# Where the weight pieces of a first mixture-of-experts loop are stored and loaded: SP's queue against ACT's queue

## The reference

```python
# block 0: 8 experts, hidden 512
h = jnp.einsum('nd,ehd->neh', xf, w1)
g = jnp.einsum('nd,ehd->neh', xf, w3)
eo = jnp.einsum('neh,edh->ned', jax.nn.silu(h) * g, w2)
out = jnp.einsum('ned,ne->nd', eo, comb)
...
# block 1: 8 experts, hidden 1024
for i in range(e):
    h = jax.nn.silu(xf @ w1[i] + b1[i])
    y = h @ w2[i] + b2[i]
    out = out + y * comb[:, i:i + 1]
```

## Time and profile before

| | us |
|---|---|
| median of 3 executions | 1332.95 (1329.78 to 1335.05) |
| the profiled execution | 1337.71 |
| its span, first to last instruction | 1336.0 |

### The profile page before, as it was taken

One profiled execution on the slowest core, in us unless ns is written; L12 is line 12 of the kernel. 1 busy time (PEld: TensorE's weight loads), 2 busy tenths in 40 slices (PEclk: granted clock), 3 DMA queues, 4 the chain that ended last, 5 costly groups with the idle time before them and its releaser, 6 DMA issues.

```text
span 1336.0 us, 26989 instructions
## 1 busy us (share of the span) xinstructions
PE 949.3 (71%) x7185; PEld 796.7 (60%) x7185; DVE 843.2 (63%) x1909; ACT 567.7 (42%) x1227; POOL 411.5 (31%) x478
## 2 busy tenths in 40 slices
PE   5210376837598888888860388457999999999943
PEld 4100265715587777777750277416888888888832
DVE  6999498898655544554545776683555555555545
ACT  5265423347575555555540023283444333443312
POOL 1285000000045444554540150003444444444310
PEclk8655596556799999999995595557999999999975
DMA  7067204913757666676677502104442442443257
GB/s 253 1 203 209 67 0 135 318 51 103 224 158 203 192 194 184 193 195 197 185 209 220 199 0 79 48 0 100 133 142 74 139 139 77 146 129 75 76 164 251
DMA packets 189423, 189.19 MB, mean 142 GB/s; under 512 B 91264, under 2 KB 158536, under 8 KB 189256
## 3 DMA queue, kind: packets, MB, share of 16 engines
q1 hardware_dynamic: 171032, 145.71, 36.6%
q0 software_dynamic: 14000, 38.82, 10.0%
q10 hardware_dynamic: 4352, 4.20, 0.9%
HBM read 119.98 MB, written 49.28 MB: 127 GB/s over the span
## 4 chain that ended last, share of the span: by engine, by line
PE 40%; DMA 29%; DVE 11%; issue 10%; ACT 4%; SPq 3%; DVEq 1%; POOLq 1%; POOL 0%; ACTq 0%
PE bank L713 15%; PE bank L735 14%; DMA region<-rows_x,fetch_now 11%; DMA xt<-region 9%; DMA wreg<-in_L_ffn_w_dram 6%; PE bank L646 4%; PE bank L563 2%; DMA wreg<-rows_y 2%; ACT xt L885 2%; PE bank L618 1%; ACT wreg L835 1%; PE bank L771 1%; DVE region L1034 1%; DVE tok L1377 1%; DVE xn L1005 1%
## 5 line engine op out<-in xcount | busy, mean ns | idle before, releaser
L713 PE MATMUL bank<-xt,wreg 128*128 x3360 | 388.3, 277 | 56.3 <-DMA xt<-region 55.7
L713 PEld LDWEIGHTS bank<-xt,wreg 128*128 128x128 f16 x3360 | 329.6, 99 | 109.4 <-issue 66.1
L735 PE MATMUL bank<-wreg,region 128*128 128x256 f16 x2520 | 286.5, 273 | 0.0
L735 PEld LDWEIGHTS bank<-wreg,region 128*128 128x128 f16 x2520 | 246.6, 98 | 28.5
L917 ACT ACTIVATE region<-bank,b_t,wreg 128x256 f32<-128x256 f32 x280 | 142.7, 560 | 227.0 <-PE bank L713 227.0
L465 POOL DMA_INDIRECT region<-rows_x,fetch_now x144 | 148.0, 1028 | 197.8 <-DMA xt<-region 132.9
L507 POOL DMA_INDIRECT rows_y<-region,put_now x140 | 139.5, 996 | 196.8 <-DVE region L1362 128.8
L1354 DVE TENSOR_SCALAR region<-region,wreg 128x512 f16<-128x512 f32 x140 | 76.4, 546 | 68.9 <-ACT region L917 66.8
L563 PE MATMUL bank<-ident,xn 128*128 128x128 f32 x256 | 54.8, 374 | 88.4 <-DVE xn L1005 82.3
L1347 DVE SCALAR_TENSOR_TENSOR region<-bank,fac,region 128x256 f32<-128x256 f32 x140 | 67.6, 483 | 72.5 <-ACT region L908 71.2
L908 ACT ACTIVATE region<-bank,fac 128x256 f32<-128x256 f32 x140 | 65.6, 469 | 107.5 <-PE bank L713 106.5
(11 more groups left out here) (238 smaller groups left out, 1191.5 us busy)
## 6 DMA issues: line engine op xcount, KB each, us to landing
wreg<-in_L_ffn_w_dram SPq DMA_DIRECT2D x138, 256.0 KB, 3.0
wreg<-in_L_ffn_w_dram SPq DMA_DIRECT2D x48, 512.0 KB, 6.2
split_v<-wreg SPq DMA_DIRECT2D x35, 512.0 KB
wreg<-split_v SPq DMA_DIRECT2D x32, 512.0 KB, 6.9
wreg<-rows_y SPq DMA_DIRECT2D x48, 256.0 KB, 3.6
rows_x<-region SPq DMA_DIRECT2D x16, 512.0 KB, 3.3
wreg<-in_x_dram SPq DMA_DIRECT2D x4, 1024.0 KB, 9.4
out_dram<-xt ACTq DMA_DIRECT2D x16, 256.0 KB, 3.7
```

Source lines behind the costliest of these rows:

```text
L713: last = pe.matmul(to, block, x_cols[:, bass.ds(b, 1), :, xs_, k, :].rearrange("p j r n -> p (j r) n"), start=(k == 0 and ws_ + xs_ == 0), ...
L735: last = pe.matmul(yb[:, r * C:(r + 1) * C], lhs[:, c, r * P:(r + 1) * P], block, start=first, stop=end, skip_group_check=True)
```

## The change

The store of a piece moves from SP's order to ACT's, one piece later, and the load of a piece moves up on SP's to right behind the transposes, one piece less ahead:

- SP iteration n: transposes of tile n+2, then two one-pass loops (the loads so far; the low part of piece n-1) instead of three, then the load of piece n+1 (before: n+2). No store. Before the loop only piece 0 is loaded (before: pieces 0 and 1).
- ACT iteration n: `split_hi(n)`, then the new `move_pieces(n)`: two one-pass loops (the store before; the low part of piece n-1) and the store of piece n-1. Then the copy of tile n's result as before. One more store follows the loop, behind a wait for the last low part.
- `piece_out` moves to another place in the same buffer. In iteration 0 the store of "piece -1" writes slot 2, which POOL has filled with zeros before the loop; the real piece 31 overwrites it later.

```diff
-        piece_out = wreg[:, 26624:29696].bitcast(F16).rearrange("p (j m s n) -> p j m s n", j=3, m=2, s=2)
+        piece_out = wreg[:, 29184:32256].bitcast(F16).rearrange("p (j m s n) -> p j m s n", j=3, m=2, s=2)
...
                     load_piece(0)
-                    sp.wait_ge(piece_loaded, 32)
-                    load_piece(1)
                 for e in range(E):
                     with sp.Fori(edges[e], edges[e + 1]) as n:
                         sp.wait_ge(z_ready[f], 4 * n + 4)
                         turn_rows(f, n + 2)
                         if f == 0:
-                            for waited, each, more in ((piece_stored, 16, 0), (piece_loaded, 32, 64), (piece_lo, 1, 1)):
+                            for waited, each, more in ((piece_loaded, 32, 32), (piece_lo, 1, 0)):
                                 with sp.Fori(n, n + 1) as m:
                                     sp.wait_ge(waited, each * m + more)
-                                    sp.sem_inc(sp_passed, 1)
-                            store_piece(n)
-                            load_piece(n + 2)
+                                    sp.sem_inc(loads_passed, 1)
+                            load_piece(n + 1)
...
-            for waited, each, more in ((piece_loaded, 32, 64), (piece_stored, 16, 0), (xc_ready[0][0], 16, 32),
+            for waited, each, more in ((piece_loaded, 32, 32), (piece_stored, 16, 16), (xc_ready[0][0], 16, 32),
...
                     pool.wait_ge(peak1_ready, 1)
+                    nc.gpsimd.memset(piece_out[:, 2].rearrange("p m s n -> p (m s n)"), 0.0)
                     spread_peaks(1)
...
+            def store_last(n):
+
+                last = (n + PIECES - 1) % PIECES
+                act.dma_start(split_v[bass.ds(last // 4, 1), :, bass.ds(last % 4 * (2 * FH[1]), 2 * FH[1])].rearrange("a p n -> p (a n)"),
+                              piece_out[:, bass.ds((n + 2) % 3, 1)].rearrange("p j m s n -> p (j m s n)")).then_inc(piece_stored, 16)
...
+            def move_pieces(n):
+
+                for waited, each in ((piece_stored, 16), (piece_lo, 1)):
+                    with act.Fori(n, n + 1) as m:
+                        act.wait_ge(waited, each * m)
+                        act.sem_inc(pieces_passed, 1)
+                store_last(n)
...
                         if f == 0:
                             split_hi(n)
+                            move_pieces(n)
                             act.wait_ge(y_ready[f], n + 1)
...
             experts(0, edges)
+            with act.Fori(edges[E], edges[E] + 1) as m:
+                act.wait_ge(piece_lo, m)
+                act.sem_inc(pieces_passed, 1)
+            store_last(edges[E])
             deviation(2)
```

More of the change, by code:

```diff
@@ L264, in bass_metaformer @@
         sum_loaded, summed, peak1_ready = [sem(f"sum_loaded{j}") for j in range(3)], sem("summed"), sem("peak1_ready")
-        v_loaded, sp_passed = sem2("v_loaded"), sem("sp_passed")
+        v_loaded, pieces_passed = sem2("v_loaded"), sem("pieces_passed")
+        loads_passed = sem("loads_passed")
         stage_loaded = sem2("stage_loaded")
@@ L273, in bass_metaformer, with load_half @@
         bias_added, conv_added = sem2("bias_added"), sem2("conv_added")
+        v1_rows, v2_rows = v1.rearrange("e (k p) f -> (e k) p f", p=P), v2.rearrange("e (q c p) d -> (e q) p c d", c=2, p=P)
+        def load_half(eng, to, m, n):
+            if m == 0:
+                return eng.dma_start(to, v1_rows[bass.ds(n // 2, 1), :, bass.ds(n % 2 * 512, 512)].rearrange("a p f -> p (a f)"))
+            return eng.dma_start(to.rearrange("p (c d) -> p c d", c=2), v2_rows[bass.ds(n, 1)].rearrange("a p c d -> p (a c) d"))
         block = ctx.enter_context(nc.Block())
@@ L297, in load_stage0 @@
                              w2[bass.ds(e, 1)].rearrange("a (c p) h -> p (a c) h", p=P)).then_inc(loaded[j], 16)
[L299 to L305, removed]
             def store_rows(f, i):
@@ L327, in _ @@
                 free(sp, summed, n - 2)
-                load_half(sum_in[:, n % 3], n % 2, n // 2).then_inc(sum_loaded[n % 3], 16)
+                load_half(sp, sum_in[:, n % 3], n % 2, n // 2).then_inc(sum_loaded[n % 3], 16)
             with sp.Fori(0, HB // 2 - 1) as h:
@@ L352, in load_piece @@
                 for m in range(2):
[L353 to L358, removed]
+                    load_half(sp, piece_in[:, bass.ds(slot, 1), m].rearrange("p j n -> p (j n)"), m, piece).then_inc(piece_loaded, 16)
             def load_v(e):
```

## The result

The changed kernel takes **1360.09 us** in the median (1356.84 to 1364.61) against 1334.00 of the kernel before beside it (1329.78 to 1336.18). The ratio is 1.0197, 95% interval 1.0165 to 1.0229: slower by 26 us. The forecast was no change, 1333 us, in a range up to 1358; the case that came is the long ring.

What follows compares the result with a forecast made beforehand. Gather and transposes bound the first loop at 19.01 us per two tiles; a new ring of 19.1 would replace them. 16 pairs gave +1.4 us, the end −1.5: no change, 1333 us, range 1312 to 1358.

Steps and rivals of the forecast that it cites:

- no change: Likeliest case for the first loop: two tiles take 18.8 to 19.5 us, time stays 1333 us; chance 0.40.
- the long ring: Rival: late piece meets other traffic, ACT's added work unhidden; two tiles take 20.7 us, +25 us, 1358 us; chance 0.30.
- The direct chain: First loop, gather, transposes, next gather: 9.5 us a tile before; taken alone after the change, 7.6 us.
- the new ring: First loop, over two tiles: transposes, late load, L893, copy, scatter, later gather, its transposes; 19.1 us against 19.01 before.
- t0: The start of a tile's transposes on SP; two tiles from one to the next took 19.01 us before.
- t0 to the second load's issue: SP, from the transposes' start to issuing the piece's second load: 2.68 + 1.17 + 0.57 = 4.42 us.
- landing and release, to L893: From the second load's issue until ACT starts the high part: landing 3.3 us, release of ACT's wait 0.59.
- L893 to the end of the copy: ACT, high part through copy of the result: 1.92 us plus 0.4 to 1.4 for added work, taken as 2.6.
- The end: SP after the last tile's transposes start: 9.6 us to its next step, 1.5 us less than before.
- all four cases: Two-tile length 18.8 to 19.5 us, chance 0.40; shorter, 0.22; PE setting the pace, 0.08; longer, 0.30.
- X: Summed length of the two-tile cycle of waits in the first loop: 19.1 us against 19.01 before.
- The third queue: ACT's queue, newly busy in the first loop, could leave the gather a smaller share; would come out as 1358 us.

Runs made afterwards that it cites:

- the fastest version: Changed kernel with pieces loaded two ahead into three slots and ACT's store behind the copy of the result: 1307.71 us, ratio 0.9819 to the kernel before.

## Why the prediction was wrong

**The mechanism held.** The gather is no longer held up: from its issue to SP's transposes it takes 3.4 us in the median of the loop for 5.1 before, the 3 to 3.7 that the prediction wanted. The direct chain is gone, and the new ring stands in its place with all its members: L893 released by the load, the scatter by the copy, the gather by POOL's own issue. The six versions without the ring (by the old lead, by a third slot, by ACT's order, by two of these) are 36 to 52 us below the change. The four that change the length of one step of it move the time the way the ring says: by 12 to 15 us where a store or a loop goes (ACT's store is 0.76 us, 16 times that is 12), and by 36 where 2.23 us are added, with PE's clock in it as said. Two signs of the prediction didn't come: two tiles take 20.3 us and not 19, and PE idles 1.6 us a tile for the 1 to 1.5 it named.

**The sum failed by its first step.** The medians of the loop's rings (33 of them, read off the timelines of SP, ACT and POOL) stand to the steps of the prediction like this:

| step | predicted, us | measured, us |
|---|---|---|
| t0 to the second load's issue | 4.42 | 5.33 |
| landing and release, to L893 | 3.89 | 4.19 |
| L893 to the end of the copy | 2.60 | 2.67 |
| to the scatter | 0.98 | 0.95 |
| scatter to gather | 3.99 | 3.71 |
| gather to t0 | 3.26 | 3.39 |
| sum of the steps | 19.1 | 20.2 |

Five steps are within 0.3 us. The first, from t0 to the second load's issue, was sized too small by 0.9, and it isn't a shift of all tiles: numbering the rings by their tile, in 14 of the 17 odd ones it is 4.5 to 4.6, near what was worked out, in 15 of the 16 even ones 5.5 to 6.8. Two rings of this kind, each over two tiles, run side by side, and what one gains at SP it loses elsewhere (the medians of gather to t0 are 3.9 us in the odd rings and 2.9 in the even ones), so both take 20.3 us. The timeline of SP shows a slow and a quick one:

```profile
446.96 2.95 SPq L348 DMA_TRANSPOSE xt<-region  x2
452.67 0.37 SPq L281 DMA_DIRECT2D wreg<-in_L_ffn_w_dram  x1
...
456.63 2.54 SPq L348 DMA_TRANSPOSE xt<-region  x2
460.58 0.36 SPq L281 DMA_DIRECT2D wreg<-in_L_ffn_w_dram  x1
```

From the transposes' end to the first load it is 452.67 − 449.91 = 2.76 us in the first and 460.58 − 459.17 = 1.41 in the second. In the chain of waits above, the 0.71 and 0.70 at 450.49 and 451.23 are the slow part: SP's own registers and branches, no wait on anything else that the profile shows. In the middle of the loop (500 to 600 us) the registers are quick, and in every second tile the second transpose of the pair waits for its gather instead, so that the pair takes 3.6 to 4.3 us for 2.54. So the step has two parts that the prediction had wrong: SP's registers, 1.17 in the sum, take 1.40 us when quick and 2.1 to 2.8 when slow, and the pair of transposes, 2.68 in the sum, waits for the gather's second half, for which the sum had no term. The prediction took one value for this step, from a tile in which three such loops went quickly, and it had no spread for it in its range.

What that is worth: the median from t0 to t0 over two tiles is 20.30 us, against 19.14 before. 17 pairs times 1.16 are 20 us. One stretch of the profiled execution is out of line, 25.6 us from the transposes at 632.12 to those at 657.76, 5 us more: a load takes 5.29 us there, and POOL idles 3.92 us ahead of the gather at 654.25 without a wait that the profile shows. A pause of this kind (4.81 us at 630.46) is in the kernel before as well. Together 25 of the 26.5.

**The end failed too, by 1.4 us.** The second load of the last tile is issued 4.52 us after t0, as worked out, but then takes 5.02 us for 3.3, in the chain of waits:

```profile
730.45 5.02 DMA wreg<-in_L_ffn_w_dram
```

The prediction had the last store out by t0 + 3 and landed before that load. It is issued at 730.40, 0.05 us before it, as ACT's timeline shows:

```profile
730.40 0.40 ACTq L885 DMA_DIRECT2D split_v<-wreg  x1
```

That the store is what made this load long is likely but only argued.

**The rival that came true did so by another sum.** The long ring was priced at 20.7 us and 1358 with ACT's added work unhidden (3.32 us) and both transfers late. ACT's work was hidden as forecast (2.67), the gather was nearly as forecast, and the landing was 0.3 later, as in that rival. The main part, 0.9 us, came from SP, whose step was the same in all cases of the prediction. With 20.3 us the prediction's own sum gives 16 × (20.30 − 19.01) − 1.5 = +19 us; the stretch out of line and the end make up the rest. That this case was among the rivals with nearly the right time is luck: its terms were others. Thus the chances were wrong in one way: all four cases shared the one step that no row showed in its new surroundings, so none of them could be long because of it.

The remaining points: the new fill of zeros on POOL took 1.80 us in its idle time of 89.7 and held no one. A gather of 2.3 us in place of 3.1 would shorten X by 0.8 us and not by half a microsecond, as the prediction has it; the 13 us beside it are right. The third queue is not what decided here: with three busy queues and two pieces ahead the kernel is at 1321.71, with two queues and the same lead at 1317.80. By the Trainium skill (DMA: Bandwidth & Descriptors, Queues, rings and completion order) each DMA engine takes turns between the queues that have work for it; a loss by a third one can't be told in these runs.

## What to carry to other kernels

A transfer that is moved to a quieter place in the order also moves its consumer's due time: write down the ring that it closes (issue, landing, consumer, what stands behind the consumer on its engine, what frees the next issue) and compare its length with the chain that is removed. If it is as long, keep the new place and give the transfer one more buffer, so that its lead is a whole iteration longer; here that turned +26 us into −14 and, with the store behind the copy, into −27. Register loops around waits are work like any other when their queue stands on the ring: merging two of them gave 12 us here, more than the loop that went.

## What the runs showed of the hardware

SP's register work between the transposes and the loads takes 1.4 us or 2 to 3 us for the same instructions. In the kernel after, the slow ones are those in which POOL issues a scatter meanwhile: all 9 stretches that meet 0.84 us or more of a scatter's issue take 2.11 to 2.76 us, and 25 of the other 26, which meet 0.2 us of one at most, take 1.38 to 1.58 (the one left over, 1.85, lies in the stretch that is out of line). POOL's timeline has a scatter inside the slow stretch above (449.91 to 452.67), and none inside the quick one (459.17 to 460.58):

```profile
450.50 0.97 POOL L501 DMA_INDIRECT rows_y<-region,put_now  x1 [0.30 <-issue]
...
461.07 1.00 POOL L501 DMA_INDIRECT rows_y<-region,put_now  x1 [5.69 <-ACT region L933]
```

The run with the zeros before the scatter separates the scatter from POOL's being busy. Two stretches of it, in the timelines of SP and of POOL: in the first (444.94 to 446.35, 1.41 us) POOL stores zeros, in the second (458.41 to 460.26, 1.85 us) it issues a scatter.

```profile
442.40 2.54 SPq L348 DMA_TRANSPOSE xt<-region  x2
446.35 0.36 SPq L281 DMA_DIRECT2D wreg<-in_L_ffn_w_dram  x1
...
454.76 3.65 SPq L348 DMA_TRANSPOSE xt<-region  x2
460.26 0.37 SPq L281 DMA_DIRECT2D wreg<-in_L_ffn_w_dram  x1
```

```profile
445.49 2.23 POOL L501 MEMSET wreg<- 128x2560 f16 x1 [4.25 <-ACT region L935]
...
457.97 1.20 POOL L503 DMA_INDIRECT rows_y<-region,put_now  x1 [0.30 <-issue]
```

All 10 stretches with 0.78 to 1.40 us of zeros in them and no scatter take 1.38 to 1.44 us; all 17 with 0.75 us or more of a scatter take 1.57 to 2.54. So POOL's zeros don't slow SP. It does not show that the scatter's issue is the cause: slow and quick ones still alternate from tile to tile in that run, the 2.1 us or more that was forecast beside a whole scatter is not always reached (1.57 us beside 0.97 us of one), and other things that happen near a scatter were not taken away.

Two other versions show that meeting a scatter is not enough. POOL issues two scatter instructions a tile, and the long overlaps above are all with the second. With only the store behind the copy, 17 stretches meet the second for over 0.4 us and take 1.86 to 3.19; of 11 that meet only the first, 7 are quick (1.38 to 1.41) and 4 take 1.71 to 1.74. With one loop on SP it is 14 (1.40 to 2.52) and 12, of which 8 are quick (1.05 to 1.07). A quick one in the timelines of the version with the store behind the copy, 493.08 to 494.48, 1.40 us, with 0.91 us of a first scatter in it:

```profile
490.54 2.54 SPq L348 DMA_TRANSPOSE xt<-region  x2
494.48 0.36 SPq L281 DMA_DIRECT2D wreg<-in_L_ffn_w_dram  x1
```

```profile
493.57 0.99 POOL L501 DMA_INDIRECT rows_y<-region,put_now  x1 [4.24 <-ACT region L932]
```

Nor is a scatter needed: in the fastest version five stretches with 1.0 us or more of a gather's issue and no scatter in them take 1.75 to 2.02 us for 1.34. Why SP is slower in these stretches stays open.
